# Masks on exponentials by a VectorE minimum, half projections and other fill slots in a five-stage attention kernel

## The chip, the cores and the metric

The kernel runs on one core of a Trainium2 chip. The metric is the device time in microseconds of one execution, the median of several. Engines are called PE (TensorE), ACT (ScalarE), DVE (VectorE), POOL (GpSimd) and SP (SyncE, which here only issues DMAs).

## What is computed

The input x is a batch of 8 sequences of 512 tokens and 256 channels, and a second tensor ctx of the same shape gives keys and values to some layers. Six attention layers follow one another. The first five have 16 heads of 16 channels each: stage 0 (keys from layer-normed ctx, an own 512x512 mask per sequence, then an MLP), stage 1 (keys from ctx, no mask that acts within the scores), stage 2 (keys from ctx, one mask for all sequences, then an MLP), stage 3 (self-attention, causal), stage 4 (keys from ctx, no mask, then an MLP). The sixth is the tail: 16 heads of 64 channels. Cut to one of the first five:

```python
q, k, v = heads(norm(x) @ wq + bq), heads(keys @ wk + bk), heads(keys @ wv + bv)
scores = einsum('bhqd,bhkd->bhqk', q, k) * 16 ** -0.5
scores = where(mask, -inf, scores)            # stages 0, 2, 3
x = x + einsum('bhqk,bhkd->bhqd', softmax(scores), v) @ wo + bo
x = x + gelu(norm(x) @ w1 + b1) @ w2 + b2     # stages 0, 2, 4
```

## The kernel before

**Units and bodies.** A unit is one sequence in one stage. The program is a chain of bodies, written per engine by `walk`. Each body works on three units at once: on `prev` it finishes the output projection (`y`), the residual and, where its stage is in `MLP`, the MLP; on `cur` it does the attention; on `nxt` it does the norm, the projections and the first row maxima. So a body whose `prev` has an MLP (an MLP body, 24 in all) differs from the others. Of the 40 bodies that have a `cur`, 16 have one of a masked stage (0 or 2): 14 of these are MLP bodies, and two (the first of either stage) are not. Nine more MLP bodies have an unmasked `cur` (the first of stages 1 and 3, seven of stage 4), and there are 14 plain bodies (seven of stage 1, seven of stage 3). In front stands a prelude without `cur`; after stage 4 come a body with only a `prev` and the tail, which the change does not touch.

**A step.** Attention is 16 steps in a body: four groups of four heads, four key tiles each. In step i PE computes the transposed scores of four heads, f32, into the four banks of `psT` (`exp_scores`, L639), adds in masked stages a penalty of -2^100 where the mask stands, by one more matmul per head with the identity as weights (L645; causal: L647), and ACT takes the exponential of two heads at a time into `probs` (L916). PE multiplies them by V one step later (`outputs`, L660), because `exp_scores` of step i has to wait until ACT has read step i-1 from `psT`.

**Maxima.** The subtracted row maxima come from a bf16 product into the two banks of `psS` (`max_scores`, L620) that DVE reduces: two 128x512 instructions that add a penalty row and take the maximum in masked and causal stages (L1087), one 128x1024 reduction elsewhere (L1090). There are 32 per unit. They run ahead of the attention by 16 or 24 (`LEADS`); `maxima_plan` says how many stand ahead of, beside and behind the other work of a step, and 16 stand inside the MLP.

**Fills.** All other products go through the single bank `small`, one fill after another: x and c (transposes of the normed x and ctx), q0, q1, k0, k1 (projections), v0, v1 (two token tiles each), m1 to m3 and m0 (maxima turned by a matmul), y0, y1, h0, h1 (transposes for the MLP), z. The tables `CUR_USES`, `Y_USES`, `NXT_USES` and so on give each fill its slot; slot 2i stands behind the scores of step i, slot 2i+1 behind its outputs. PE may write a fill only after an engine has read the one before: ACT takes x, c, h, q, k (L938, L947, L951), DVE takes v, m, y (L1108, L1110, L1114, L1120).

**Other queues.** ACT turns the uint8 masks of stage 0 into bf16 penalties (`penalties`, L955): one set at slot 17 or 15, one at the very end of the body. SP issues the loads of a body in order, then stores the heads' outputs, gathers them with their sums, and after DVE's reciprocal (slot 5) spreads the reciprocals (L472, L477); POOL then scales the gathered outputs (L1345), which y0 waits for.

## Time and profile before

| what | us |
|---|---|
| median of 3 runs (5240.43 to 5261.33) | 5246.33 |
| the profiled execution | 5242.84 |
| its span | 5241.0 |
| a typical stage 0 body (window 416 to 537) | 121 |
| a typical stage 1 body (window 1248 to 1315) | 67 |
| stage 4, five MLP bodies (window 3262 to 3810) | 548 |
| the tail (window 3970 to 5241) | 1271 |

A row of the timeline gives the start, the length, the engine and line, the operation with its tiles, and in square brackets how long the engine had been idle and what released it. A group row gives busy time, the mean of one instruction in ns, and behind the bar the idle time ahead of such instructions with its releasers. A matmul row counts two instructions for one f32 product.

### The profile page before, as it was taken

How to read it: one execution, taken by the hardware profiler on the slowest of the kernel's cores; microseconds unless marked ns; L12 is line 12 of the kernel's file. 1: busy time of each engine (PE TensorE's matmuls, PEld its weight loads, DVE VectorE, ACT ScalarE, POOL GpSimd, SP SyncE). 2: the span in 40 equal slices, each digit the busy share in tenths (PEclk: the TensorE clock that was granted, in tenths of full speed). 3: DMA queues.
4: the chain of work that ended last, by engine and by line, in shares of the span. 5: the costliest groups of instructions: out<-in, count | busy, mean ns of one | idle time of the engine just before them, and what ended most of it. 6: DMA issues, size and time to landing. Idle time of an engine off the chain costs nothing.

```text
span 5241.0 us, 69325 instructions
## 1 busy us (share of the span) xinstructions
PE 4666.1 (89%) x24708; PEld 1851.2 (35%) x24708; DVE 2678.7 (51%) x6305; ACT 2286.7 (44%) x2870; POOL 919.6 (18%) x831
## 2 busy tenths in 40 slices
PE   5899999898888999999888888888867999999999
PEld 2333333332332333343433333333333333333333
DVE  5544554457676444454455565444422545554554
ACT  3444444456564444434444444444432433333332
POOL 0111111101110111001111111110111433333333
PEclk8999999999999999999999999999988999999999
DMA  1111111121121100001111211110111000000000
GB/s 57 33 42 45 41 49 49 35 71 66 56 69 46 40 30 31 30 29 40 65 59 57 68 63 43 41 35 33 37 42 52 1 13 13 13 13 13 1 13 9
DMA packets 152319, 201.89 MB, mean 39 GB/s; under 512 B 18993, under 2 KB 102321, under 8 KB 150706
## 3 DMA queue, kind: packets, MB, share of 16 engines
q1 hardware_dynamic: 151986, 197.31, 11.1%
q8 instruction: 226, 3.70, 0.3%
q14 instruction: 107, 0.88, 0.1%
HBM read 128.86 MB, written 68.42 MB: 38 GB/s over the span
## 4 chain that ended last, share of the span: by engine, by line
PE 69%; issue 11%; DVE 9%; ACT 7%; DMA 2%; POOL 1%; SPq 1%; ACTq 0%; DVEq 0%; POOLq 0%
PE psT L639 8%; PE small L592 7%; PE psT L717 6%; PE psO L660 6%; PE small L599 6%; PE psS L620 6%; PE psT L859 4%; ACT probs L916 4%; PE psT L645 3%; PE psT L726 3%; PE small L726 3%; DVE out L1087 3%; PE psT L592 2%; PE psT L824 2%; PE psO L874 2%
## 5 line engine op out<-in xcount | busy, mean ns | idle before, releaser
L916 ACT ACTIVATE probs<-psT 128x1024 f32<-128x1024 f32 (+3 forms) x1280 | 1158.9, 958 | 1150.7 <-PE psT L645 541.4
L1090 DVE TENSOR_REDUCE nmb<-psS 128x2 bf16<-128x1024 f32 x512 | 627.5, 1226 | 438.6 <-PE psS L620 438.3
L639 PE MATMUL psT<-low 32*128 32x512 f32 (+3 forms) x5120 | 744.7, 610 | 103.3 <-ACT probs L916 74.6
L1087 DVE CUSTOM_DVE_ANT_0 out<-psS,pens_sb 128x512 f32<-128x512 f32 x1024 | 665.8, 688 | 106.3 <-issue 68.6
L620 PE MATMUL psS<-out 32*128 32x512 bf16 (+3 forms) x2560 | 485.8, 376 | 253.5 <-DVE nmb L1087 104.1
L660 PE MATMUL psO<-probs,V 128*32 128x512 f32 (+3 forms) x5120 | 664.0, 592 | 1.0 <-ACT probs L916 1.0
L1272 DVE TENSOR_REDUCE parts<-psS 128x2 bf16<-128x1024 f32 x256 | 314.9, 1230 | 522.1 <-PE psS L846 522.1
L1027 ACT ACTIVATE probs<-psT 128x1024 f32<-128x1024 f32 x256 | 262.0, 1023 | 526.1 <-PE psT L862 526.1
L620 PEld LDWEIGHTS psS<-out 32*128 32x128 bf16 x2560 | 121.3, 91 | 979.9 <-issue 330.7
L717 PE MATMUL psT<-out,W 128*128 128x512 f32 x768 | 382.3, 618 | 0.2
L1084 DVE MEMSET scratch<- 128x1 f32 x768 | 45.3, 59 | 636.0 <-PE psS L620 611.9
L1389 POOL TENSOR_TENSOR oN<-oN,probs 128x1024 f32<-128x1024 f32 x128 | 300.6, 2349 | 316.1 <-ACT probs L1027 315.8
L947 ACT ACTIVATE low<-small,vec 128x512 f32<-128x512 f32 x320 | 222.7, 748 | 229.9 <-PE small L592 228.3
L639 PEld LDWEIGHTS psT<-low 32*128 32x128 f32 x5120 | 236.4, 188 | 192.1 <-ACT probs L916 131.0
L1338 POOL TENSOR_TENSOR var<-mhalf 128x4 f32<-128x4 f32 x80 | 15.9, 198 | 1593.2 <-ACT low L947 1593.2
L859 PE MATMUL psT<-V 64*128 64x512 f32 x1024 | 290.0, 643 | 2.2 <-ACT parts L1017 1.0
L645 PE MATMUL psT<-pens_sb,identb 128*128 128x512 bf16 x1024 | 276.6, 394 | 0.0
L1087 DVE CUSTOM_DVE_ANT_0 out<-psS,tri_row 128x384 f32<-128x384 f32 (+3 forms) x512 | 230.4, 487 | 80.2 <-issue 69.6
L1114 DVE TENSOR_TENSOR low<-low,small 128x512 f32<-128x512 f32 x160 | 109.8, 687 | 303.7 <-PE small L699 301.9
L592 PE MATMUL small<-hT,Wqkv 128*128 128x512 f32 x448 | 226.6, 629 | 37.1 <-ACT hT L938 23.9
L961 ACT ACTIVATE gel<-psT,vec 128x512 f32<-128x512 f32 x192 | 131.9, 687 | 250.7 <-PE psT L717 250.4
L1389 POOL TENSOR_TENSOR oN<-probs 128x1024 f32<-128x1024 f32 x64 | 150.5, 2351 | 422.9 <-ACT probs L1027 422.9
(156 smaller groups left out, 5555.9 us busy)
## 6 DMA issues: line engine op xcount, KB each, us to landing
o_mid<-out SPq DMA_DIRECT2D x160, 256.0 KB, 2.0
oN<-o_mid SPq DMA_DIRECT2D x160, 128.0 KB
oN<-r_mid SPq DMA_DIRECT2D x80, 256.0 KB
x_mid<-xe SPq DMA_DIRECT2D x40, 512.0 KB, 2.9
xw<-x_mid SPq DMA_DIRECT2D x36, 512.0 KB, 4.1
xe<-x_mid SPq DMA_DIRECT2D x36, 512.0 KB, 4.8
cT<-ctxT SPq DMA_DIRECT2D x20, 512.0 KB, 4.2
W<-wm SPq DMA_DIRECT2D x6, 1024.0 KB, 8.1
```

What stands on the lines that cost most here:

```text
L592: last = nc.tensor.matmul(dst[:], w[:, c, cols], src[:, c, :], start=c == 0, stop=c == C - 1)
L620: last = nc.tensor.matmul(psS[e][:, 0:n], Qb[rows_of(j), q, a, c, qt * P:(qt + 1) * P], Kb[rows_of(j), q, c, 0:n], start=True, stop=True)
L639: last = nc.tensor.matmul(psT[j][:, q0:S], Kf[rows_of(j), q, a, c, kt * P:(kt + 1) * P], Qf[rows_of(j), q, a, c, q0:S], start=True, stop=p ...
L645: last = nc.tensor.matmul(psT[j], identb[:], pens[:, 1, kt * S:(kt + 1) * S], start=False, stop=True)
L660: last = nc.tensor.matmul(psO[32 * j:32 * j + 32, q0:S], V[:, u.parity, kt, head(g, j), :], probs[:, i % 2, j, q0:S], start=kt == 0, stop= ...
L717: last = nc.tensor.matmul(psT[m % 2], W1[:, c, m * P:(m + 1) * P], hM[:, c, :], start=c == 0, stop=c == C - 1)
L859: nc.tensor.matmul(psT[j], K5[n % 3][rows, kt * P:(kt + 1) * P], Q5[n % 3][rows, :], start=True, stop=False)
L916: nc.scalar.activation(probs[:, i % 2, two, q0:S], psT_all[:, two, q0:S], ACT.Exp, scale=float(DH) ** -0.5)\
L1087: nc.vector.tensor_tensor_reduce(junk[:, e, 0:n], psS[e][:, 0:n], penalty, 1.0, -3.0e38, ALU.add, ALU.max, nmb4[:, g % 2, qt, at:at + 1]). ...
L1090: nc.vector.tensor_reduce(nmb4[:, g % 2, qt, row:row + 33:32], psS_both[:, :, 0:n], AX, ALU.max)\
L1272: nc.vector.tensor_reduce(nmb[n % 2][:, qt, 0:P:DL], psS_both[:], AX, ALU.max, negate=True).then_inc(tail_s_read, 1)
L1389: nc.gpsimd.tensor_tensor(pacc[n % 2], before, P5[kt], ALU.add).then_inc(tail_summed, 1)
```

## The change

- `exp_scores`: in masked stages PE computes heads 2 and 3 first and signals them without a penalty; heads 0 and 1 follow and get theirs. Only two of four penalty matmuls remain. Causal steps keep all four.
- `limit` (DVE, new): the exponentials of heads 2 and 3 (128x1024 f32 in SBUF) are replaced by the minimum of themselves and a bf16 tile `lims` that is e^-64 where the mask stands and e^64 elsewhere. It stands at the head of DVE's next step, and `outputs` waits for it (semaphore `limited`). `limits` (ACT, new) makes the tile with one 128x2048 Exp.
- `outputs` of masked stages stand behind the late fills of their step.
- The penalties and the limit tile of stage 0 are made at slots 3, 5 and 7 in two buffers; the mask loads wait for three of them.
- Fills: q and k of non-MLP bodies come in two halves of 256 tokens each (q00, q01, ...); v comes as four fills of one token tile, two of them (v2, v3) in the next body at slots 1 and 3; y of non-MLP bodies comes as four single tiles; m1, m2, m3, m0, x0, x1 move, h0 and h1 are taken by DVE instead of ACT; in MLP bodies the maxima of step 12 stand beside and behind instead of ahead and beside. The row maxima have a buffer per group.
- SP: the loads of Wqkv and of cT wait until v3 has been taken, and stand behind the gather and ahead of `spread_recips`.

```diff
-CUR_USES = {True: {"m1": 1, "m2": 11, "m3": 17}, False: {"m1": 1, "m2": 10, "m3": 21}}
-Y_USES = {True: {"y0": 10, "y1": 12}, False: {"y0": 17, "y1": 19}}
-MLP_USES = {"h0": 18, "h1": 19, "z": 19.5}
-CTX_USES = {True: {"c0": 13, "c1": 14}, False: {"c0": 12, "c1": 12}}
-NXT_USES = {True: {"x0": 7, "x1": 8, "q0": 9, "k0": 16, "q1": 21, "m0": 22, "k1": 23, "v0": 25, "v1": 27},
-            False: {"x0": 7, "x1": 9, "q0": 11, "k0": 13, "q1": 23, "m0": 25, "k1": 27, "v0": 29, "v1": 31}}
-MASKS_AT = {True: 17, False: 15}
+CUR_USES = {True: uses_at("0 m1, 1 v2, 3 v3, 4 m2, 20 m3"), False: uses_at("0 m1, 1 v2, 3 v3, 12 m2, 20 m3")}
+Y_USES = {True: uses_at("10 y01, 12 y23"), False: uses_at("14 y0, 15 y1, 17 y2, 19 y3")}
+MLP_USES = uses_at("18 h0, 19 h1")
+CTX_USES = {True: uses_at("13 c0, 14 c1"), False: uses_at("10 c0 c1")}
+NXT_USES = {True: uses_at("6 x0, 7 x1, 9 q0, 16 k0, 21 q1, 23 k1, 24 m0, 27 v0, 29 v1"),
+            False: uses_at("6 x0, 7 x1, 9 q00, 10 q01, 11 k00, 13 k01, 21 q10, 23 q11, 25 k10, 26 m0, 27 k11, 29 v0, 31 v1")}
+MASKS_AT = (3, 5, 7)
...
-        last = (1, 1, 0) if out > IN_BLOCK else (0, 0, 0)
-        return [(0, 0, 0)] + 8 * [(1, 0, 0)] + 3 * [(0, 0, 0)] + 4 * [last]
+        last = [(0, 1, 1)] + 3 * [(1, 1, 0)] if out > IN_BLOCK else 4 * [(0, 0, 0)]
+        return [(0, 0, 0)] + 8 * [(1, 0, 0)] + 3 * [(0, 0, 0)] + last
...
-X_STATS, X_NORMALISE = (2, 3), (5, 6)
-C_STATS, C_NORMALISE = {True: (8, 9), False: (7, 8)}, {True: (11, 12), False: (10, 11)}
+X_STATS, X_NORMALISE = (2, 3), (5, 5)
+C_STATS, C_NORMALISE = {True: (8, 9), False: (6, 7)}, {True: (11, 12), False: (9, 10)}
...
+                if cur is not None and (new_keys or new_stage):
+                    wait_taken(sp, place, "cur", "v3")
+                if new_stage:
+                    sp.dma_start(Wqkv[:], wa[nxt.s, :, 0:N_QKV]).then_inc(qkv_in, 16)
+                if new_keys:
+                    sp.dma_start(cT[:], keys).then_inc(sem["ctx_in"], 16)
...
-                for j in range(4):
+                for j in (2, 3, 0, 1) if u.s in MASKED else range(4):
+                    plain = u.s != CAUSAL and not (u.s in MASKED and j < 2)
                     last = nc.tensor.matmul(psT[j][:, q0:S], Kf[rows_of(j), q, a, c, kt * P:(kt + 1) * P], Qf[rows_of(j), q, a, c, q0:S],
                                             start=True, stop=plain)
...
-                for j in range(4):
+                for j in range(2 if u.s in MASKED else 4 if u.s == CAUSAL else 0):
...
+                if i in (2, 3):
+                    wait_taken(pe, place, "cur", f"v{i}")
                 pe.wait_ge(sem["exp_done"], count("exp_done", u, 2 * i + 2))
+                if u.s in MASKED:
+                    pe.wait_ge(sem["limited"], count("limited", u, i + 1))
...
-                    long = any(use[0] in "qkvyw" for _, use in late)
+                    long = any(use in ("q0", "q1", "k0", "k1", "w") for _, use in late)
...
-                    if i == 0 and prev is not None:
-                        outputs(prev, STEPS - 1)
-                    if i > 0 and cur is not None and not after_mlp:
-                        outputs(cur, i - 1)
+                    of = prev if i == 0 else None if after_mlp else cur
+                    limited = of is not None and of.s in MASKED
+                    if of is not None and not limited:
+                        outputs(place, of, (i - 1) % STEPS)
...
                     for owner, use in late:
                         fill(place, owner, use, prev, cur, nxt)
+                    if limited:
+                        outputs(place, of, (i - 1) % STEPS)
...
-                if kind not in "xchqk":
+                if kind not in "xcqk":
...
+            def limits(u):
+                return nc.scalar.activation(masking(lims, u), masks[:, 1, :], ACT.Exp, bias=log_limit[:, 0:1], scale=-2.0 * LOG_LIMIT)
...
+                    if nxt is not None and nxt.s == 0 and slot == MASKS_AT[1]:
+                        score_penalties(nxt).then_inc(sem["pens"], 1)
+                    if nxt is not None and nxt.s == 0 and slot == MASKS_AT[2]:
+                        limits(nxt).then_inc(sem["pens"], 1)
...
-                if nxt is not None and nxt.s == 0:
-
-                    penalties(1).then_inc(sem["pens"], 1)
...
+            def limit(u, i):
+
+                dve.wait_ge(sem["exp_done"], count("exp_done", u, 2 * i + 1))
...
+                two, row = probs[:, i % 2, 2:4, :], masking(lims, u)[:, i % T * S:(i % T + 1) * S]
+                both = bass.AP(tensor=row.tensor, offset=row.offset, ap=[list(row.ap[0]), [0, 2], list(row.ap[1])])
+                nc.vector.tensor_tensor(two, two, both, ALU.min).then_inc(sem["limited"], 1)
...
                 for i, (before, beside, after) in enumerate(place.body.maxima()):
+                    of = prev if i == 0 else None if place.body.mlp and i == MLP_AFTER + 1 else cur
+                    if of is not None and of.s in MASKED:
+                        limit(of, (i - 1) % STEPS)
                     maxima(before)
```

## Rows read from the trace of the kernel before

**Rows 1.** The page: busy time of each engine.

```profile
PE 4666.1 (89%) x24708; PEld 1851.2 (35%) x24708; DVE 2678.7 (51%) x6305; ACT 2286.7 (44%) x2870; POOL 919.6 (18%) x831
```

**Rows 2.** Windows: length, busy PE, PEld, DVE, ACT, POOL, then granted clock, DMA.

```profile
416.00:537.00 121.00, 109.58 (x572) 45.47 (x576) 59.70 (x210) 56.78 (x65) 13.90 (x19) 0.98 0.12 41
...
1248.00:1315.00 67.00, 58.10 (x389) 20.10 (x388) 47.36 (x56) 40.80 (x48) 8.73 (x11) 1.00 0.19 65
...
1597.00:1694.00 97.00, 80.52 (x468) 27.16 (x469) 59.97 (x220) 41.27 (x48) 8.72 (x11) 0.95 0.17 56
...
3262.00:3810.00 548.00, 473.75 (x2480) 195.54 (x2478) 262.86 (x345) 249.34 (x300) 66.31 (x89) 0.98 0.11 38
```

**Rows 3.** Groups by line in the window 177 to 891, six masked MLP bodies.

```profile
L639 PE MATMUL psT<-low 32*128 32x512 f32 x768 | 114.6, 635 | 20.3 <-ACT pens_sb L955 11.8 <-ACT probs L916 7.6 <-DVE V L1110 0.7
...
L645 PE MATMUL psT<-pens_sb,identb 128*128 128x512 bf16 x384 | 103.7, 394 | 0.0
...
L620 PE MATMUL psS<-out 32*128 32x512 bf16 x386 | 75.0, 385 | 16.1 <-ACT out L951 12.6 <-DVE nmb L1087 3.5
...
L592 PE MATMUL small<-hT,Wqkv 128*128 128x512 f32 x48 | 23.8, 618 | 7.5 <-ACT hT L938 5.5 <-DVE xe L1152 2.0
...
L955 ACT ACTIVATE pens_sb<-out 128x2048 bf16<-128x2048 uint8 x12 | 23.0, 1917 | 0.0
L599 PE MATMUL small<-Wo,oN 128*128 128x256 f32 x96 | 23.0, 382 | 1.0 <-POOL oN L1345 1.0
...
L587 PE MATMUL small<-ident,xn 128*128 128x128 f32 x96 | 15.1, 280 | 5.4 <-ACT out L938 5.4
...
L1345 POOL TENSOR_TENSOR oN<-oN 128x1024 f32<-128x1024 f32 x6 | 14.1, 2350 | 56.3 <-DMA oN<-r_mid 56.3
...
L699 PE MATMUL small<-identb,nmb 128*128 128x128 bf16 x96 | 9.7, 225 | 6.2 <-ACT out L951 6.2
```

**Rows 4.** PE's timeline from the start of the body at 417.9.

```profile
417.90 1.14 PE L639 MATMUL psT<-low 32*128 32x512 f32 x8 [2.46 <-ACT pens_sb L955]
418.97 1.04 PE L645 MATMUL psT<-pens_sb,identb 128*128 128x512 bf16 x4
419.94 1.06 PE L660 MATMUL psO<-probs,V 128*32 128x512 f32 x8
...
425.39 1.14 PE L639 MATMUL psT<-low 32*128 32x512 f32 x8 [0.28 <-ACT probs L916]
...
429.18 1.14 PE L639 MATMUL psT<-low 32*128 32x512 f32 x8 [0.36 <-ACT probs L916]
```

**Rows 5.** Groups by form, DVE, whole span.

```profile
L1087 DVE CUSTOM_DVE_ANT_0 out<-psS,pens_sb 128x512 f32<-128x512 f32 x1024 | 665.8, 688 | 106.3 <-issue 68.6 <-DVE nmb L1087 36.7 <-DVE nmb L1090 0.6
...
L1131 DVE TENSOR_TENSOR valid<-valid,vtmp 128x512 f32<-128x512 f32 x1 | 0.7, 691 | 0.0
```

**Rows 6.** Timeline, SP and PE: the reciprocals are sent, and y0 starts.

```profile
428.48 0.34 SPq L472 DMA_DIRECT2D r_mid<-rsum  x1
...
441.39 1.89 PE L599 MATMUL small<-Wo,oN 128*128 128x256 f32 x8
```

**Rows 7.** PE's timeline in the window 3262 to 3375, stage 4.

```profile
3273.24 1.14 PE L639 MATMUL psT<-low 32*128 32x512 f32 x8 [0.79 <-ACT probs L916]
...
3280.40 1.98 PE L592 MATMUL small<-hT,Wqkv 128*128 128x512 f32 x4 [1.19 <-ACT hT L938]
3285.68 1.99 PE L599 MATMUL small<-Wo,oN 128*128 128x256 f32 x8 [2.12 <-POOL oN L1345]
...
3353.99 0.39 PE L620 MATMUL psS<-out 32*128 32x512 bf16 x2 [2.19 <-ACT out L951]
```

**Rows 8.** PE's timeline at the start of a plain stage 1 body.

```profile
1250.17 0.39 PE L620 MATMUL psS<-out 32*128 32x512 bf16 x2 [1.59 <-DVE V L1108]
...
1251.89 0.39 PE L620 MATMUL psS<-out 32*128 32x512 bf16 x2 [0.45 <-DVE nmb L1090]
```

**Rows 9.** The instructions that read `rstd`: duration ns min/median/max.

```profile
L1067 DVE TENSOR_SCALAR xn<-xw,mom,rstd x160: 390/410/860, 19.2 to 3714.7; 128x256 f32<-128x256 f32 x160
```

More of the change, by code:

```diff
@@ L178, in start, with named, first, last @@
         return self.i * self.step + self.before
+    def named(self, who, begins):
+        return [use for _, owner, use in self.body.uses if owner == who and use.startswith(begins)]
+    def first(self, who, begins):
+        return self.named(who, begins)[0]
+    def last(self, who, begins):
+        return self.named(who, begins)[-1]
 def schedule():
@@ L530, in _ @@
             sp.dma_start(W2[:], wm2[0]).then_inc(wm_in, 16)
-            for n, fills in enumerate(walk(sp, body)):
+            for n, _ in enumerate(walk(sp, body)):
                 s, kind = divmod(n - 1, 3)
-                if n >= 1 and s < 4 and kind == 1:
-                    sp.wait_ge(small_read, fills + 1)
-                    sp.dma_start(Wqkv[:], wa[s + 1, :, 0:N_QKV]).then_inc(qkv_in, 16)
                 if n >= 1 and s < 5 and kind == 0:
@@ L667, in fill @@
                 dst = small
-                kind, part = use[0], use[1:]
+                kind = use[0]
                 if kind == "x":
@@ L675, in fill @@
                     pe.wait_ge(sem["normed_m"], count("normed_m", u, 1))
-                if use == "k0" and u.s not in OWN_KEYS and u.s:
+                if kind == "k" and use == place.first(who, "k0") and u.s not in OWN_KEYS and u.s:
                     pe.wait_ge(sem["ctx_in"], count("ctx_in", u, 16))
                 if kind == "m":
-                    pe.wait_ge(sem["s_read"], count("s_read", u, 2 * T * (int(part) + 1) * reads(u.s)))
-                if use == "q0":
+                    pe.wait_ge(sem["s_read"], count("s_read", u, 2 * T * (int(use[1]) + 1) * reads(u.s)))
+                if kind == "q" and use == place.first(who, "q0"):
                     pe.wait_ge(qkv_in, 16 * (u.s + 1))
-                if use == "y0":
+                if kind == "y" and use == place.first(who, "y"):
                     pe.wait_ge(wo_in, 16 * (u.s + 1))
@@ L929, in take @@
                 u = {"prev": prev, "cur": cur, "nxt": nxt}[who]
-                kind, part = use[0], use[1:]
-                if kind not in "xchqk":
+                kind = use[0]
+                if kind not in "xcqk":
                     return
@@ L1195, in between, with mlp @@
                         normalise(1, xe, xn, halves(1)).then_inc(sem["normed_m"], 1)
-            def mlp(place, u, nxt):
+            def mlp(place, u, cur, nxt):
+                if cur is not None and cur.s in MASKED:
+                    limit(cur, MLP_AFTER)
                 for n in range(IN_BLOCK):
```

167 lines of the change are left out of this document (95 added, 72 removed).

## The prediction

> **What bounds the kernel now.** I read the page's busy times first: PE works for 4666.1 of the span's 5241.0 us, 89%, DVE half of it, ACT less [rows 1]. So PE is the path, and a change is worth what it takes off PE plus what it takes off PE's waits. The windows show that this holds in every kind of body, unequally [rows 2]: a masked MLP body has PE busy 109.6 of 121 us, a plain stage 1 body 58.1 of 67, the first body of stage 2 80.5 of 97, five bodies of stage 4 473.8 of 548. Then the groups of six masked MLP bodies, for what ends PE's waits [rows 3]: 20.3 us ahead of the scores (ACT making penalties or still at its exponentials), 16.1 ahead of the maxima, 7.5 + 1.0 + 5.4 + 6.2 ahead of fills, mostly for ACT to read `small`: 56.5 us, 9.4 per body. The timeline shows where steps carry no fill: scores 425.39, next scores 429.18, a period of 3.79 us with 0.36 of waiting, set by ACT's round, not by PE's work [rows 4].
>
> **The change, part by part.**
>
> *Penalties.* Two of four matmuls go in each of 16 x 16 = 256 masked steps. Four take from 418.97 to 419.94, so 0.2425 each by spacing [rows 4]; the group's 103.7 us for 384 gives 0.27 [rows 3]. I take 0.24, full-clock spacing: 0.48 a step, 7.7 a body. In the 14 masked MLP bodies PE is the path: 14 x 7.7 = -108. In the two masked bodies without MLP it mostly waits for DVE (16.5 of 97 us idle [rows 2]), so I count nothing there yet.
>
> *The minimum.* No row has a 128x1024 DVE operation with two SBUF inputs. Nearest is L1131, 128x512 f32 with both inputs in SBUF, 0.691 [rows 5]; twice that, 1.38, is a bound from above on its own engine. Adding 512 elements to L1087's pace is no less than 0.53 more (0.69 less a fixed part), so I take 1.2. From far above stands POOL's 128x1024 multiply of two SBUF tiles, 2.35 [rows 3]; from below 0.69, if the bf16 operand doubled the rate, for which no row speaks. DVE goes from 59.7 to 59.7 + 16 x 1.2 + 1.4 (two h takes) = 80 in a body of about 115. That fits, in sum. Queue order decides: `limit` of step i-1 stands at DVE's head of step i and needs only the first exponentials of step i-1, which finish a step earlier; the outputs that wait for it come after the scores and fills. In steps 1 to 8 one maximum (2 x 0.69 [rows 5]) and one limit a step leave room. Behind the MLP there are eight maxima in four steps: each then waits for a reduction with a limit in front.
>
> *Walk of a masked MLP body*, with 1.2 per limit, 1.38 per maximum, the other engines at their present pace, and the orders of the code; waits of PE that I get: step 0, v2 behind m1, which DVE takes after a limit, 0.8. Step 3, x1 must wait until ACT took x0, behind exponentials and (stage 0) a 1.92 penalty set [rows 3]: 1.9. y01: the reciprocals come at the end of a DVE stretch that now holds limits, v3, m2 and the whole normalisation, some 2.2 later after the scores of step 1 than now, while PE arrives 0.4 earlier; now y0 starts 12.9 after the reciprocals are sent, with almost no wait [rows 6], so 2.6. c0 right behind y23, without outputs between (seven bodies): 0.85. h1 behind h0: 0.85, as now. m3 and q1 behind the MLP: 0.3 + 0.8, against 0.3 (xe [rows 3]) and 0.6 now. Steps 12 to 15: m0 hides the take of k1, but the maximum behind step 12 and that ahead of step 13 stand back to back with a limit between: 0.55 + 1.5, then three of 0.6: 3.9, against 2.1 + 0.6 now (12.6 and 3.5 over six bodies [rows 3]). Gone is the 2.46 at the start of a body behind the penalties, and the 0.28 and 0.36 of steps 2 and 3 [rows 4], because the three new ACT sets lie under steps that now carry v3, m2, x0, x1. Sum 11.7 for stage 0, about 10.5 for stage 2; against 9.4, +2.3 with rounding up for stage 0: 14 x 2.3 = +32.
>
> *The two masked bodies without MLP.* They have 40 maxima; DVE busy is 60 of 97 [rows 2] and gets 19 more, in a chain where PE and DVE take turns. 79 plus the turns comes to about the present length: 7.7 less on PE and as much more waiting, 0, with -4 to +6 each.
>
> *Unmasked MLP bodies (9).* PE work stays. v2 and v3 fall into steps that wait 0.79 for ACT [rows 7]: -1.4. x0, x1 earlier take away q0's 1.19; y0's 2.12 shrinks by about 1 since 1.9 us of v stand ahead, though the reciprocals come 0.7 later; m2 at slot 4 and DVE taking h0 save about what the groups show for them in stage 0, 1.0 and 0.9 [rows 3]. Added: x1 0.65, q1 behind m3 0.8, the back-to-back maxima, while the 2.19 behind k1 [rows 7] falls to 1.0: +0.3 for the end. About -4; for hand-overs that I cannot see I take -3: -27.
>
> *Plain bodies (14).* One turn of maximum and reduction takes 1.72 (1250.17 to 1251.89 [rows 8]). A step has two gaps between maxima, about 1.15 (scores) and 1.4 (outputs and a maximum) of work [rows 4, 8]; each without a fill costs the rest. Half fills cover more gaps, but the long ones covered a gap with 1.9 of work that needed no cover; counting slots, 6.3 of waiting against 5.8. The 1.59 behind the V takes [rows 8] goes, as one tile takes DVE half; hand-overs of halves cost about 0.5, each half being read by ACT in instructions that cost more than half of a whole. -0.7 each: -10.
>
> *SP, POOL, prelude.* cT and Wqkv now wait for v3 and are issued with the reciprocals behind them. v3 is read at slot 3, the reciprocals come at slot 5, k0 and q0 later: hidden; were v3 late, the reciprocals and y would be. Mask loads wait for three sets, done at slot 7, well before SP arrives. POOL keeps its work; its scaling, late as computed, comes before the rstd of c, which DVE wants after y01: hidden. Prelude: one penalty set of 1.92 [rows 3] leaves the path ahead of the maxima and one joins it ahead of x0: 0. DMA volume is unchanged.
>
> Sum: -108 + 32 + 0 - 27 - 10 = -113. Against the profiled execution's 5242.84 (3.5 under the median of 5246.33, so no different within the runs): 5130.
>
> **A rule weighed.** The normalisation of xw has a median of 0.41 us but reaches 0.86 [rows 9], and POOL is at work for 13.9 us of a masked body [rows 2]; so DVE operations from SBUF can be stretched by up to 0.45 by something, with 16 limits a body added to them. If each of them paid that, DVE would get 7.2 a body more; PE's waits follow where DVE ends them, in about half of the steps: +3.6, times 16, +58. The Trainium skill, "SBUF — State Buffer", section "Who interferes with whom", says that a DVE instruction with two SBUF inputs and a GpSimd instruction that reads SBUF exclude each other for their whole length. By that rule the time would come out as in the second rival; the stretched normalisation fits it.
>
> **Rivals.**
> 1. *PE's waits go, too.* My walk assumes that DVE reaches each item as late as its queue allows. If the 3.9 at the end and the 2.6 at y01 don't arise, 14 x 6.5 = 91 more is gained: 5039. For it: every wait in rows 3 is short, and DVE idles half of the body. Against: eight maxima and four limits in four steps.
> 2. *The limits and POOL get in each other's way*, +58: 5188.
> 3. *Hand-overs of the halves.* Six further fills in 16 bodies without MLP cost a take each, as q0's 1.19 [rows 7] less its hiding, 0.9: 16 x 6 x 0.9 = +86 to 5216, and with half of rival 2 to 5245: no change that can be told.
> 4. *Slower: the limit takes 2.35, as POOL's operation of that shape does* [rows 3]. Then DVE has 99 of 115 us in a masked body and every step hangs on it: 1.15 x 16 more in DVE's row, 0.65 of it on the path in each step, 10 a body, and all 18 in the two others: 14 x 10 + 36 = 176, 5306. It decides from about 1.9 us per limit. For it only that row; against it L1131's 0.691 for half.
>
> The change does what it says: the dropped matmuls are 512 by the code.
>
> **How the numbers follow.** Forecast 0.50, rival 1 0.22, rival 2 0.15, rival 3 0.06, rival 4 0.07. A measurement here can tell about 0.5%, 26 us, so faster means under 5220: forecast, rivals 1 and 2: 0.87; same 0.06; slower 0.07. The forecast's own range is 5085 to 5180 (0.22 to 0.27 for a penalty matmul, -4 to +6 for the two bodies, 3 us a body on the walk). The range reaches from rival 1's value to a little over rival 2's, 5035 to 5200, and leaves out rivals 3 and 4 and the outer part of rival 1, 0.19.
>
> **What would show it.** The penalty group in the form 128x512 bf16 with 512 fewer instructions; a new DVE group of 256, about 1.2 us each; stage 0 bodies about 5 us shorter, stage 4 bodies 3 shorter, stage 1 within 1; no wait for penalties ahead of the scores; waits ahead of y01, and ahead of the maxima behind the MLP. I am wrong if the DVE group runs over 1.9, if outputs wait for it, or if masked bodies shrink by less than 2 or more than 9 us.

## The result and the profile after

| | before | after |
|---|---|---|
| median, us | 5249.88 (14 runs, 5240.43 to 5261.50) | 5230.91 (14 runs, 5217.12 to 5239.33) |
| the profiled execution | 5242.84 | 5238.51 |
| its span | 5241.0 | 5236.7 |
| mean granted clock of the span | 0.973 | 0.959 |

The ratio is 0.9962, interval 0.9953 to 0.9971: 19 us gained. The gain is small but clear of the scatter of the runs; it is within the 26 us that the prediction took as the least that can be told. 120 us were forecast (5130, range 5035 to 5200), so the prediction was wrong.

One sentence ahead of the prediction needs correction: by the code's `OWN_KEYS = (2, 3)` stages 2 and 3 both take their keys from x, so ctx feeds stages 0, 1 and 4, and a load of `cT` belongs to the units of stages 1 and 4.

The page of after: its busy line, the granted clock in 40 slices, and two of the groups.

```profile
PE 4648.7 (89%) x24484; PEld 1877.5 (36%) x24484; DVE 3017.8 (58%) x6690; ACT 2310.5 (44%) x3011; POOL 963.7 (18%) x831
...
PEclk9999999999999999999999999999988999999999
...
L1154 DVE TENSOR_TENSOR probs<-probs,parts 128x1024 f32<-128x1024 f32 x256 | 315.5, 1232 | 59.8 <-ACT probs L966 51.4
...
L642 PE MATMUL small<-Wo,oN 128*128 128x256 f32 x640 | 188.5, 435 | 81.8 <-POOL oN L1416 48.9
```

PE is busy 17 us less than in [rows 1], not 123, though DVE got what was forecast for it (+339: 316 of minima at 1.23 us each, and the takes of h). To see where, I cut both spans at the issues of the DMA that gathers the sums, one per body, 6 to 13 us into it. The windows of after, then of before; the columns are those of [rows 2]. In order: seven masked MLP bodies of stage 0; the first body of stage 1; seven plain bodies of stage 1; the first of stage 2; seven masked MLP bodies of stage 2; the first of stage 3; seven plain bodies of stage 3; the first of stage 4; seven MLP bodies of stage 4. Of before five of the nine are shown.

```profile
193.39:999.58 806.19, 728.64 (x3739) 300.25 (x3732) 550.98 (x1491) 381.49 (x436) 117.83 (x131) 0.96 0.13 42
999.58:1109.65 110.07, 93.58 (x481) 38.64 (x483) 47.24 (x67) 53.15 (x61) 12.72 (x17) 0.95 0.20 68
1109.65:1610.67 501.02, 434.00 (x2862) 165.78 (x2861) 341.93 (x482) 307.31 (x407) 61.02 (x77) 0.98 0.19 61
1610.67:1710.70 100.03, 77.08 (x460) 28.24 (x464) 78.43 (x240) 45.01 (x60) 10.66 (x11) 0.95 0.13 43
1710.70:2500.39 789.69, 719.55 (x3707) 293.41 (x3700) 525.80 (x1531) 345.79 (x407) 108.55 (x120) 0.97 0.10 35
2500.39:2598.18 97.79, 85.65 (x553) 42.17 (x551) 39.81 (x176) 38.21 (x58) 12.47 (x16) 0.97 0.19 66
2598.18:3058.77 460.59, 398.67 (x3289) 191.94 (x3292) 281.33 (x1218) 223.89 (x406) 61.08 (x77) 0.94 0.19 61
3058.77:3149.48 90.71, 73.34 (x426) 26.64 (x418) 55.37 (x64) 42.42 (x58) 8.74 (x11) 0.85 0.16 54
3149.48:3901.52 752.04, 655.32 (x3358) 272.82 (x3354) 347.82 (x468) 330.78 (x393) 88.26 (x117) 0.94 0.12 38
```

```profile
185.43:1011.79 826.36, 760.94 (x3970) 313.62 (x3962) 412.37 (x1363) 382.67 (x446) 96.16 (x131) 0.99 0.13 41
...
1119.17:1605.78 486.61, 426.63 (x2756) 150.03 (x2753) 344.45 (x472) 287.56 (x337) 61.11 (x77) 0.97 0.18 62
1605.78:1702.08 96.30, 80.17 (x476) 26.98 (x474) 59.12 (x217) 41.46 (x49) 8.72 (x11) 0.96 0.13 45
1702.08:2512.43 810.35, 750.09 (x3930) 308.20 (x3922) 388.99 (x1406) 355.59 (x422) 89.63 (x120) 0.99 0.10 34
...
3162.47:3908.12 745.65, 637.05 (x3348) 264.89 (x3348) 330.95 (x435) 338.99 (x405) 88.13 (x117) 0.98 0.11 38
```

The account of the two profiled executions, in us:

| bodies | forecast | came, by the windows | cut at the first scores |
|---|---|---|---|
| 14 masked MLP | -76 | (806.19 - 826.36) + (789.69 - 810.35) = -40.8 | -38.2 |
| 9 unmasked MLP | -27 | +2.7 (first of stage 1), -4.2 (first of stage 3), +6.4 (stage 4) = +4.9 | +1.5, -3.0, +7.8 = +6.3 |
| 14 plain | -10 | +14.4 (stage 1), -0.2 (stage 3) = +14.2 | +17.2, +0.2 = +17.4 |
| first of stages 0 (with the prelude), 2 and 4 | 0 | +8.0, +3.7, +3.4 = +15.1 | +4.9, +1.2, +2.0 = +8.1 |
| the rest | 0 | +2.3 | +2.3 |
| sum | -113 | -4.3 | -4.3 |

The last column cuts at the first scores of each body instead (179.05 before and 183.90 after for the second body of stage 0). It differs because the gather moves within the body: 6.4 us behind these scores in that body before, 9.5 after. So a row can be off by some 3 us, which matters for the single bodies more than for the stretches of seven.

**In masked MLP bodies** PE is busy 4.6 us less per body of stage 0 (32.3 / 7) and 4.4 of stage 2, where 7.7 was forecast, and idle 1.7 and 1.4 more (9.3 to 11.1, 8.6 to 10.0), where 2.3 was. The groups of PE in the seven bodies of stage 0, after, then before:

```profile
L682 PE MATMUL psT<-low 32*128 32x512 f32 x898 | 142.6, 657 | 5.2 <-issue 5.1
...
L663 PE MATMUL psS<-out 32*128 32x512 bf16 x450 | 90.0, 397 | 21.3 <-DVE nmb L1141 18.4 <-DVE nmb L1144 2.7
...
L688 PE MATMUL psT<-out,identb 128*128 128x512 bf16 x124 | 38.8, 396 | 0.0
L642 PE MATMUL small<-Wqkv,cT 128*128 128x256 f32 x112 | 36.6, 456 | 5.5 <-DVE low L1178 5.5
L688 PE MATMUL psT<-pens_sb,identb 128*128 128x512 bf16 x96 | 30.3, 399 | 0.0
```

```profile
L639 PE MATMUL psT<-low 32*128 32x512 f32 x896 | 133.6, 633 | 23.5 <-ACT pens_sb L955 14.0 <-ACT probs L916 9.3
...
L645 PE MATMUL psT<-pens_sb,identb 128*128 128x512 bf16 x440 | 118.2, 393 | 0.0
...
L620 PE MATMUL psS<-out 32*128 32x512 bf16 x450 | 87.4, 385 | 18.6 <-ACT out L951 14.7 <-DVE nmb L1087 3.5 <-DVE nmb L1090 0.3
...
L599 PE MATMUL small<-Wqkv,cT 128*128 128x256 f32 x112 | 27.9, 392 | 0.0
```

The penalties fell nearly as computed, from 118.2 to 38.8 + 30.3 us: 49 in seven bodies, 7.0 each. But the same scores take 9.0 more and the same 112 matmuls of v take 8.7 more, 456 ns each and not 392. The granted clock of these bodies went from 0.99 to 0.96. Not all of v's part belongs to the clock: in best2 (below), which has the new slots and a clock of 0.99, they take 32.1 us, so 4.2 of the 8.7 come with fills of one tile. The waits are others: ACT's 23.5 ahead of the scores is 5.2 now, and what ends the waits ahead of maxima and fills is mostly DVE. PE's timeline of after around the end of a stage 0 body, and below it the windows of the same stretch (PE's columns and, third from the end, the clock):

```profile
393.93 0.39 PE L663 MATMUL psS<-out 32*128 32x512 bf16 x2 [0.70 <-DVE nmb L1141]
395.89 0.61 PE L663 MATMUL psS<-out 32*128 32x512 bf16 x2 [1.57 <-DVE nmb L1141]
...
413.39 2.09 PE L682 MATMUL psT<-low 32*128 32x512 f32 x8 [2.58 <-issue]
...
417.65 2.07 PE L642 MATMUL small<-Wqkv,cT 128*128 128x256 f32 x4 [0.78 <-DVE low L1178]
```

```profile
394.00:397.00 3.00, 1.43 (x8) 0.76 (x12) 2.52 (x8) 0.00 (x0) 0.00 (x0) 0.70 0.45 129
397.00:400.00 3.00, 3.00 (x13) 0.59 (x6) 1.33 (x6) 1.74 (x2) 0.00 (x0) 0.50 1.02 350
...
412.00:415.00 3.00, 1.61 (x8) 0.52 (x8) 1.22 (x1) 0.00 (x0) 0.00 (x0) 0.54 0.03 8
415.00:418.00 3.00, 2.22 (x11) 1.00 (x8) 0.69 (x1) 1.94 (x2) 0.00 (x0) 0.50 0.00 0
```

Scores that take 1.14 us in [rows 4] take 2.09 at 413.39, at the 1.2 GHz level: the clock fell behind the 0.70 and 1.57 of waiting for maxima, and again behind the 2.58 at the start of the body. The second drop is not new, as before's body at 417.90 starts behind a wait of 2.46 [rows 4]. The first has grown. Windows of 3 us, each below full clock counted as (1 - clock) x 2 x its length, give the time at the lower level in seven masked MLP bodies:

| kernel | stage 0, us (per body) | stage 2, us (per body) |
|---|---|---|
| before | 20.5 (2.9) | 13.7 (2.0) |
| after | 68.3 (9.8) | 54.6 (7.8) |
| best1 (below) | 37.5 (5.4) | 37.5 (5.4) |
| best2 (below) | 20.5 (2.9) | 23.9 (3.4) |

In stage 0 a body spends 6.8 us more at half speed, some 3.4 us of work not done. By its size that covers the 3.1 which the 4.6 lacks against 7.7.

The start of the body is better than it looks in that one timeline. Before, units 2 to 7 of stage 0 (counted from 0) all begin behind a wait of 2.2 to 2.5 us for penalties, the 14.0 us of the group above. After, only units 3 and 5 do, 2.58 and 2.50 us with `issue` as the cause, the 5.1 above.

### The profile page after: what moved, and what is told of

Read it like the earlier page. It is cut to its first block, busy times and chain, and to the rows that moved or that the text cites. A ratio compares the mean times of both kernels' runs of the same rounds, so it can differ in the third digit from the quotient of the medians.

```text
span 5236.7 us, 70053 instructions
## 1 busy us (share of the span) xinstructions
PE 4648.7 (89%) x24484; PEld 1877.5 (36%) x24484; DVE 3017.8 (58%) x6690; ACT 2310.5 (44%) x3011; POOL 963.7 (18%) x831
## 4 chain that ended last, share of the span: by engine, by line
PE 64%; DVE 14%; issue 12%; ACT 4%; DMA 4%; POOL 1%; SPq 1%; DVEq 0%; ACTq 0%; POOLq 0%
PE psO L707 7%; PE small L635 7%; PE psT L764 6%; PE small L642 6%; PE psS L663 6%; PE psT L682 5%; PE psT L908 4%; DVE out L1141 3%; PE psT L773 3%; PE small L773 3%; DVE nmb L1144 3%; PE psT L635 2%; PE psT L873 2%; PE psO L923 2%; PE psT L642 2%
## 5 line engine op out<-in xcount | busy, mean ns | idle before, releaser
L682 PE MATMUL psT<-low 32*128 32x512 f32 (+3 forms) x5120 | 771.7, 621 | 49.7 <-ACT probs L966 28.2
L663 PE MATMUL psS<-out 32*128 32x512 bf16 (+3 forms) x2560 | 494.1, 383 | 219.1 <-DVE nmb L1141 121.4
L996 ACT ACTIVATE low<-small,vec 128x256 f32<-128x256 f32 (+1 forms) x464 | 262.2, 617 | 204.2 <-PE small L635 204.2
L1154 DVE TENSOR_TENSOR probs<-probs,parts 128x1024 f32<-128x1024 f32 x256 | 315.5, 1232 | 59.8 <-ACT probs L966 51.4
L682 PEld LDWEIGHTS psT<-low 32*128 32x128 f32 x5120 | 252.2, 192 | 145.8 <-issue 77.7
L635 PE MATMUL small<-hT,Wqkv 128*128 128x256 f32 (+1 forms) x656 | 242.9, 494 | 24.2 <-DVE low L1178 18.7
L642 PE MATMUL small<-Wo,oN 128*128 128x256 f32 x640 | 188.5, 435 | 81.8 <-POOL oN L1416 48.9
```

The source lines that it names most:

```text
L635: last = nc.tensor.matmul(dst[:, tokens], w[:, c, cols], src[:, c, tokens], start=c == 0, stop=c == C - 1)
L642: last = nc.tensor.matmul(dst[:, i * D:(i + 1) * D], src[:, c, t * P:(t + 1) * P], w[:, c, :], start=c == 0, stop=c == n - 1)
L663: last = nc.tensor.matmul(psS[e][:, 0:n], Qb[rows_of(j), q, a, c, qt * P:(qt + 1) * P], Kb[rows_of(j), q, c, 0:n], start=True, stop=True)
L682: last = nc.tensor.matmul(psT[j][:, q0:S], Kf[rows_of(j), q, a, c, kt * P:(kt + 1) * P], Qf[rows_of(j), q, a, c, q0:S], start=True, stop=p ...
L1154: nc.vector.tensor_tensor(two, two, both, ALU.min).then_inc(sem["limited"], 1)
```

## The experiments

All runs were compared with the kernel before on the same chip (medians 5252.6, 5255.3 and 5254.4 in three sessions). Each profile is one execution, and not always a middling one: after's is 7.6 us above its median, those of keys_behind and maxima_apart are 19 and 14 us below theirs. The lengths of bodies, in us, worked out from their profiles as above (stretches of seven divided by seven); where a slash stands, PE's idle time per body follows:

| bodies | before | after | before_two_pen | slots_only | limit_none | mask_only | dummy | best1 | best2 |
|---|---|---|---|---|---|---|---|---|---|
| prelude and first | 185.4 | 193.4 | 184.1 | 180.6 | 182.2 | 187.0 | 198.9 | 192.8 | 185.4 |
| stage 0 MLP | 118.1 / 9.3 | 115.2 / 11.1 | 116.4 / 13.4 | 115.0 / 6.1 | 114.5 / 11.0 | 119.3 / 16.1 | 121.0 / 8.6 | 113.1 / 10.8 | 113.1 / 5.1 |
| stage 1 plain | 69.5 | 71.6 | 69.2 | 71.0 | 71.0 | 69.0 | 71.6 | 71.9 | 70.8 |
| stage 2 first | 96.3 | 100.0 | 90.1 | 93.0 | 92.9 | 97.7 | 108.3 | 98.2 | 90.2 |
| stage 2 MLP | 115.8 / 8.6 | 112.8 / 10.0 | 113.9 / 12.7 | 115.4 / 6.5 | 111.3 / 9.7 | 119.3 / 16.3 | 120.0 / 7.5 | 111.6 / 10.1 | 113.2 / 5.5 |
| stage 3 plain | 65.8 | 65.8 | 66.0 | 65.7 | 65.8 | 66.1 | 65.7 | 65.4 | 65.3 |
| stage 4 MLP | 106.5 | 107.4 | 107.1 | 108.2 | 107.4 | 109.1 | 107.0 | 104.4 | 103.7 |

### The penalties alone, without a minimum or new slots

```diff
 # kernel before
-                plain = u.s not in (*MASKED, CAUSAL)
+                    plain = u.s != CAUSAL and not (u.s in MASKED and j < 2)
-                for j in range(4):
+                for j in range(2 if u.s in MASKED else 4):
```

(The signals for both pairs of heads follow the second penalty. So ACT starts on the first pair no sooner than before; in after it starts behind two scores.)

> The kernel before with the penalties of heads 2 and 3 left out and nothing in their place (their scores are not masked). It prices the removed matmuls alone. Theory 'clock': 512 matmuls at 0.24 us take 123 us off PE's row, but PE's waits keep their length and become a larger share, so the granted clock falls under 0.97 and a part is given back: 5150 to 5190. Rival 'waits alone': the clock stays at 0.97 and the whole 123 us come out: about 5127.

5218.33, ratio 0.9931 [0.9903, 0.9958]: 34 us gained of some 123, less than either theory had. The window of the seven stage 0 MLP bodies, and their scores:

```profile
184.07:998.55 814.48, 720.72 (x3746) 292.66 (x3742) 412.31 (x1361) 380.66 (x446) 96.15 (x131) 0.98 0.13 42
```

```profile
L639 PE MATMUL psT<-low 32*128 32x512 f32 x896 | 137.6, 653 | 36.8 <-ACT probs L918 21.4 <-ACT pens_sb L957 15.3
```

PE is busy 5.7 us less per body than before (40.2 / 7), idle 4.1 more, 28 in seven. Of these 28 us, 13.3 stand ahead of the scores (23.5 to 36.8), nearly all for ACT's exponentials (9.3 to 21.4); the rest stand ahead of fills and maxima, half of them for ACT as well. Over the whole span the waits ahead of the scores for `probs` rise from 74.6 to 100.6 us. So taking matmuls away uncovers ACT, whose round [rows 4] show for steps without a fill and which I had not carried into the term for the penalties. No minimum, no new slot and no other queue is touched here. But the first pair's signal stays where it was, so this run alone does not tell what after's new order of the pairs could have freed; the run without the minimum, below, does.

### The new slots alone

```diff
 # kernel after
-                for j in (2, 3, 0, 1) if u.s in MASKED else range(4):
-                    plain = u.s != CAUSAL and not (u.s in MASKED and j < 2)
+                for j in range(4):
+                    plain = u.s not in (*MASKED, CAUSAL)
...
-                if u.s in MASKED:
-                    pe.wait_ge(sem["limited"], count("limited", u, i + 1))
...
-                    limited = of is not None and of.s in MASKED
+                    limited = False
...
-                if cur is not None and cur.s in MASKED:
-                    limit(cur, MLP_AFTER)
```

(And the other call of `limit`, and ACT's order of the pairs.)

> The changed kernel with four penalty matmuls, no minimum, and outputs ahead of the late fills in every stage: the new slots and halves alone. Theory 'the slots cost in unmasked stages' (stage 1 and stage 4 bodies 2 us longer, as in the changed kernel): 5250 to 5280. Rival 'the minimum spoils it, the slots help': 5200 to 5230.

5230.32, ratio 0.9958 [0.9945, 0.9970]: the same as after. With the new tables the swap of two penalties a step for a minimum is worth nothing; it makes the masked MLP bodies 0.1 longer in stage 0 and 2.5 shorter in stage 2, and costs 12.8 in the prelude with the first body and 7.0 in the first body of stage 2 (9.7 and 4.3 if cut at the first scores).

### The minimum alone

```diff
 # kernel after, with the tables of the kernel before
-CUR_USES = {True: uses_at("0 m1, 1 v2, 3 v3, 4 m2, 20 m3"), False: uses_at("0 m1, 1 v2, 3 v3, 12 m2, 20 m3")}
+CUR_USES = {True: uses_at("1 m1, 11 m2, 17 m3"), False: uses_at("1 m1, 10 m2, 21 m3")}
...
-                    wait_taken(sp, place, "cur", "v3")
+                    sp.wait_ge(small_read, place.start() + 1)
```

(`Y_USES`, `CTX_USES`, `NXT_USES`, `maxima_plan` and the slots of the norms likewise. Three further parts of after stay: DVE takes h, the mask sets are made at slots 3, 5 and 7, and the outputs stand behind the late fills. SP's loads keep their new place behind the gather.)

> The changed kernel with the slots, whole projections, plan of maxima and order of normalisation of the kernel before, but with the minimum, half of the penalties and outputs behind fills. Theory 'the slots cost in unmasked stages': the unmasked stages have their old times, the masked bodies gain: 5190 to 5215, under the changed kernel. Rival 'the slots make room for the minimum': masked bodies gain nothing, 5240 to 5270.

5298.76, ratio 1.0085 [1.0060, 1.0111]: 46 us slower than before, which neither theory had. Masked MLP bodies idle 16 us. Not all of it is the minimum's: of the 59 us between the two profiled executions, 33 stand in the masked MLP bodies and 18 in stage 4, which has no minimum, so that part belongs to what else stays. Still, the slots are not an extra of the change but what makes the minimum bearable: slots alone 22 us faster, minimum without them 46 slower, both 19 faster.

### Idle work in place of the penalties

```diff
 # kernel after
+                if u.s in MASKED:
+                    for j in range(2):
+                        nc.tensor.matmul(psT[j], identb[:], masking(pensE, u)[:, kt * S:(kt + 1) * S], start=True, stop=True)
```

> The changed kernel with two idle 128x512 bf16 matmuls put back into each masked step, into banks that the scores overwrite (512 in all, 123 us of PE work). Theory 'clock': in masked bodies the granted clock rises from about 0.96 to 0.98 or more and the added work costs clearly less than itself, 40 to 80 us: 5270 to 5310. Rival 'the clock is no matter': the work adds in full, 5340 to 5355.

5343.21, ratio 1.0171 [1.0145, 1.0196]: 112 us slower than after, nearly the full 123. The clock of the stage 0 MLP bodies rose from 0.96 to 0.98, yet PE's busy time rose by 8.3 a body (787 against 729 in seven), more than the added 7.7. So a fuller PE does not pay for itself with its clock. And adding work costs nearly all of it while removing as much from before gave a third. That fits steps which stand near the point where PE's work and the round of the other engines are equal, a point that a row of busy times doesn't show. The two runs are not mirror images, though: the idle matmuls stand ahead of the scores, where they delay both pairs of exponentials, and the removed ones stood behind the first pair's signal. Idle work at that place was not tried.

### After without the minimum

```diff
 # kernel after
-                if u.s in MASKED:
-                    pe.wait_ge(sem["limited"], count("limited", u, i + 1))
...
-                if cur is not None and cur.s in MASKED:
-                    limit(cur, MLP_AFTER)
...
-                    if of is not None and of.s in MASKED:
-                        limit(of, (i - 1) % STEPS)
```

> The changed kernel without the minimum and without the wait for it (heads 2 and 3 stay unmasked); all else as it is. It prices the 256 minima. Theory 'DVE's queue': the waits of PE at fills that DVE reads and at the maxima behind the MLP shrink by 2 to 3 us a masked body and the granted clock there rises to 0.98: 5170 to 5195. Rival 'hidden': 5220 to 5235.

5202.61, ratio 0.9903 [0.9880, 0.9927]: the minimum costs 28 us by the medians. The first body of stage 2:

```profile
1591.93:1684.86 92.93, 76.33 (x468) 27.81 (x470) 60.66 (x226) 45.37 (x60) 8.68 (x11) 0.96 0.14 47
```

Against after that is 7.1 us less, with DVE busy 60.7 and not 78.4; the prelude with the first body loses 11.1. The masked MLP bodies lose only 0.7 (stage 0) and 1.5 (stage 2) each. In bodies with an MLP the minimum is nearly hidden; in the two without one, where DVE's 40 maxima and PE take turns, 0.44 to 0.70 us of each of the 16 minima lie on the path.

Beside slots_only this run prices the penalties once more, now in the new slots and with the first pair of heads signalled behind two scores: neither has a minimum, and one makes four penalties a step, the other two (the outputs stand behind the late fills in this one). The ratios to before are 0.9958 and 0.9903, 29 us for the same 512 matmuls: 0.6 us a body in stage 0 and 4.0 in stage 2. PE is busy 5.4 us less a body in stage 0 and idle 4.8 more. With this, -108 is out for the new order of the pairs as well.

### Half and whole fills

```diff
 # kernel after
-False: uses_at("14 y0, 15 y1, 17 y2, 19 y3")
+False: uses_at("17 y01, 19 y23")
...
-False: uses_at("6 x0, 7 x1, 9 q00, 10 q01, 11 k00, 13 k01, 21 q10, 23 q11, 25 k10, 26 m0, 27 k11, 29 v0, 31 v1")
+False: uses_at("6 x0, 7 x1, 11 q0, 13 k0, 23 q1, 26 m0, 27 k1, 29 v0, 31 v1")
```

> The changed kernel with q, k and y of the bodies without MLP whole again, in the slots of the kernel before; v stays in four tiles. Theory: each further fill costs PE about 0.1 to 0.15 us of restart and a hand-over: plain bodies 1.5 to 2 us shorter (71.6 to 70 in stage 1): 5195 to 5210. Rival: the halves were needed to cover the maxima: 5230 to 5250.

5250.76, ratio 0.9988 [0.9975, 1.0001]: 20 us worse than after. Plain bodies of stage 1 gain 1.2 (70.4), those of stage 3 lose 3.7 (69.5). The halves have a price and a use. The price stands in the groups of seven plain bodies, first before, then after:

```profile
L592 PE MATMUL small<-hT,Wqkv 128*128 128x512 f32 x64 | 31.7, 618 | 0.0
```

```profile
L635 PE MATMUL small<-hT,Wqkv 128*128 128x256 f32 x128 | 36.2, 405 | 0.5 <-ACT low L996 0.5
```

By busy time a half takes 0.283 us and half of a whole would be 0.248 (the means, 405 and 618 ns, include overlap): 4.5 us more for these, and 3.3 for k's products out of `cT`, in the same windows (23.8 to 27.1). y and v, which come a tile at a time, take 3.7 and 5.9 more. Other groups got shorter, so PE's busy time rose by 7.4 us in all (434.0 against 426.6); in this run, with v still in tiles, it is 422.0. The use is in stage 3, whose whole fills in the new slots uncover 3.7 us a body. Halves in stage 3 and wholes in stage 1 were not tried.

### Reciprocals ahead of the normalisation

```diff
 # kernel after, in DVE's `between`
+                if prev is not None and slot == RECIP_AT:
+                    reciprocals(prev)
...
-                if prev is not None and slot == RECIP_AT:
-                    reciprocals(prev)
```

> The changed kernel with DVE's reciprocals of slot 5 ahead of the normalisation instead of behind it. Theory: in MLP bodies PE waits at y01 for POOL's scaling (4.2 us in stage 4) and runs several us at half clock behind that wait; sent 2.65 us earlier, the wait shrinks by as much and the clock holds: 2 to 4 us a body in 23 MLP bodies, 5140 to 5185. Rival: x0 now waits longer for the norm, and the clock falls anyway: 5215 to 5235.

5229.63, ratio 0.9954 [0.9936, 0.9972]: nothing, and the wait of y for POOL is 49.3 us on the whole, as in after (48.9). The SP rows of one stage 4 body tell why; before, after, this kernel and the next one, keys_behind (the load of the keys `cT`, the gather of the outputs `oN<-o_mid`, the write of the reciprocals, their spread `oN<-r_mid`, which waits until the write has landed):

```profile
3365.26 0.37 SPq L512 DMA_DIRECT2D cT<-ctxT  x1
...
3384.08 2.33 SPq L467 DMA_DIRECT2D oN<-o_mid  x4
3388.14 0.34 SPq L472 DMA_DIRECT2D r_mid<-rsum  x1
3392.20 1.24 SPq L477 DMA_DIRECT2D oN<-r_mid  x2
```

```profile
3373.27 2.24 SPq L507 DMA_DIRECT2D oN<-o_mid  x4
3375.80 0.38 SPq L561 DMA_DIRECT2D cT<-ctxT  x1
3380.29 0.35 SPq L512 DMA_DIRECT2D r_mid<-rsum  x1
3383.23 1.25 SPq L517 DMA_DIRECT2D oN<-r_mid  x2
```

```profile
3363.82 2.23 SPq L507 DMA_DIRECT2D oN<-o_mid  x4
3366.35 0.38 SPq L561 DMA_DIRECT2D cT<-ctxT  x1
3368.00 0.35 SPq L512 DMA_DIRECT2D r_mid<-rsum  x1
3373.89 1.25 SPq L517 DMA_DIRECT2D oN<-r_mid  x2
```

```profile
3350.01 2.24 SPq L507 DMA_DIRECT2D oN<-o_mid  x4
3356.87 0.34 SPq L512 DMA_DIRECT2D r_mid<-rsum  x1
3358.34 1.25 SPq L517 DMA_DIRECT2D oN<-r_mid  x2
```

In after and in this kernel the spread goes out 7.4 and 7.5 us behind the load of `cT`, whether the small write is issued 4.5 or 1.7 us behind that load. Counted from the start of the gather (512 KB in four DMAs), the four bodies give 8.1, 10.0, 10.1 and 8.3 us, with the write sent 4.1, 7.0, 4.2 and 6.9 us behind it. The other bodies of before say the same: the write is sent 2.3 to 6.8 us behind the gather, and the spread follows the gather by 7.9 to 8.8. By these numbers the small write is waited for until what was queued ahead of it is through: the gather, in every kernel, and a load between the two adds 1.9 us. Sending the write earlier helps nothing.

### Keys behind the reciprocals

```diff
 # kernel after, MLP bodies
-                if new_keys:
+                if new_keys and not late_keys:
                     sp.dma_start(cT[:], keys).then_inc(sem["ctx_in"], 16)
...
+                if late_keys:
+                    if cur is not None:
+                        wait_taken(sp, place, "cur", "v3")
+                    sp.dma_start(cT[:], keys).then_inc(sem["ctx_in"], 16)
```

> The changed kernel with the load of cT (512 KB) in MLP bodies behind spread_recips instead of ahead of it. Theory: the write of the reciprocals lands only when the load ahead of it in the queue is through, 7.4 us after its issue; behind it, the scaling comes 3 to 4 us earlier in the eight MLP bodies whose next unit reads ctx (six of stage 4), y01 waits 1 us or none and the clock holds: stage 4 bodies 107.4 to about 103, total 5190 to 5207. Rival: POOL's scaling is late for other reasons, 5222 to 5235.

5226.60 (10 runs, 5207.99 to 5247.28), ratio 0.9946 [0.9930, 0.9963]. The stage 4 bodies fall from 107.4 to 105.2, and y's wait for POOL from 48.9 to 35.2 us on the whole. In stage 4 alone the wait went from 13.2 us before to 24.6 after, 1.9 for each of six bodies, and is 16.2 here. The mechanism is there, at 1.9 us a body and not the 3 to 4 expected; the whole time moved by 4 us only, within the intervals of the two.

### The maxima behind the MLP, and the first combination

```diff
 # kernel after
-        last = [(0, 1, 1)] + 3 * [(1, 1, 0)] if out > IN_BLOCK else 4 * [(0, 0, 0)]
+        last = 4 * [(0, 1, 1)] if out > IN_BLOCK else 4 * [(0, 0, 0)]
```

> The changed kernel with the maxima of steps 12 to 15 of MLP bodies all beside and behind, (0,1,1) four times, so that none stand back to back. Theory: the waits of 0.7 and 1.57 us and the half clock behind them go, 1.5 to 3 us a body in 21 bodies: 5170 to 5200. Rival: DVE paces these steps, the waits only move: 5220 to 5240.

5213.73, ratio 0.9920 [0.9904, 0.9937]: 17 us better than after. Stage 0 MLP bodies fall to 113.1, stage 4's to 105.4. The 1.57 shown above, a maximum directly behind another with a minimum between them on DVE, is what this order takes away: PE's waits ahead of maxima for DVE's masked reductions fall from 121.4 to 99.2 us over the span.

This order, the reciprocals first and whole fills together:

> The changed kernel with the three edits together: reciprocals first, maxima apart, whole q, k and y. If they are independent their gains add: by the theories about 5231 - 70 - 45 - 30 = 5085, at least 5150. Rival (each wait removed uncovers the next one): 5190 to 5230.

5220.79, ratio 0.9941 [0.9920, 0.9962]: worse than the order alone, as stage 3 loses 2.7 a plain body (68.5) again.

### Two versions for speed

Keys behind, maxima apart and reciprocals first, in one kernel:

> The changed kernel with three edits: cT behind the reciprocals, reciprocals ahead of the normalisation, maxima (0,1,1) behind the MLP. Theory: with cT out of the way the earlier reciprocals count, too: 5231 - 17 - 30 - 15 = 5170. Rival (no gain beyond the maxima): 5210.

5192.37, ratio 0.9878 [0.9849, 0.9906]: 38 us better than after, where the three alone gave 4, 17 and 1. What the other 16 come from is not settled (by the ratios to before, 44 against 8, 22 and 4, it is 10).

The same with four penalties a step and without the minimum (the edits of the slots alone):

> As best1, but with four penalty matmuls and no minimum. It tells what the minimum is worth once the other waits are gone. Theory: removing 123 us of PE work is worth 15 to 40 us only: 5185 to 5210. Rival (the minimum is worth nothing in net): equal to best1.

5170.64, ratio 0.9838 [0.9812, 0.9864]: 84 us below before by the medians, the fastest, and under what either theory had. Its windows of the seven MLP bodies of stages 0 and 2:

```profile
185.41:977.39 791.98, 756.37 (x3965) 314.10 (x3961) 420.57 (x1385) 383.79 (x437) 95.59 (x131) 0.99 0.13 43
...
1676.12:2468.34 792.22, 753.43 (x3930) 309.75 (x3929) 398.07 (x1418) 346.53 (x408) 88.67 (x119) 0.98 0.11 35
```

PE is busy as much as before (756 against 761 us in stage 0) at the same granted clock, and idle 5.1 us a body, not 9.3. Against best1 the MLP bodies are equal in stage 0 and 1.6 longer in stage 2; the prelude with the first body is 7.4 shorter and the first body of stage 2 8.0 (5.2 and 5.5 if cut at the first scores). The seven plain bodies of stage 1 and the seven of stage 4, which no minimum touches, are 12 us shorter in this profile too, for a reason that was not looked for. So the gain lay in the slots, and on top of the best of them the title's main part costs 22 us by the medians, of which its two bodies without an MLP show some 11.

## Why the prediction was wrong, step by step

- **Penalties, -108.** The step that failed first. The work that leaves is right: 7.0 us a body by the groups, 7.7 forecast. That "in the 14 masked MLP bodies PE is the path" is wrong downward: taken out of before alone, the work gave 34 us in place of 123, 1.7 and 1.8 a masked MLP body, and PE's idle time took up 4.1 of the 5.7 that it was busy less. In the new slots it gave 29. I had read the 0.36 and 3.79 of [rows 4] as a matter of steps without a fill and treated 7.7 as a pure gain in all of them.
- **PE's busy time at a constant clock.** 0.24 "full-clock spacing" was also taken as if the other matmuls kept theirs. They took 17.7 us more in seven bodies for scores and v alone; 4.2 of it came with v's smaller fills, the rest while the granted clock fell from 0.99 to 0.96. 6.8 us a body more at half speed, 3.4 of work, match the 3.1 between the 7.7 and the 4.6. The walk priced each wait at its length, and a wait that the clock follows costs more.
- **Walk of waits, +2.3 a body.** Near in size: +1.7 and +1.4 (its terms add up to 12.0, not 11.7). Several places fit as well: v2 behind m1 waits 0.78 (0.8 forecast), the maxima behind the MLP 0.70 and 1.57 (0.55 and 1.5). Others were wrong and made up for each other, so the sum owes something to luck: y01 waits 0.2 to 1.5 us in units 1 to 6 of stage 0 and not 2.6, with 4.9 in unit 7 alone; and the wait at the start of the body went in four of the six bodies that had it, and stayed in units 3 and 5.
- **The two masked bodies without MLP, 0, with up to +6.** They and the first of stage 4, which I had left out, came to +15, or +8 cut at the first scores. The run without the minimum puts 18 us of cost on the two (17 by that cut). "79 plus the turns comes to about the present length" was the error: in a chain of turns an instruction on one side adds itself, and the saved PE work did too little against it.
- **Unmasked MLP bodies, -27.** Came +4.9. "k0 and q0 later: hidden" looked at who reads the new keys. The load's harm was to what stands behind it in SP's order: the reciprocals, then POOL, then y, 1.9 us a body in stage 4. The prediction named the wait ahead of the load and not the load ahead of the write. "PE work stays" failed too: in stage 4 PE's idle time did fall, by 1.7 us a body where 3 was forecast, but its busy time rose by 2.6, with the clock at 0.94 and not 0.98 and v in single tiles.
- **Plain bodies, -10.** Came +14.2, all in stage 1. I priced the halves' takes at 0.5 and nothing for PE; PE is busy 7.4 us more in seven bodies, half of it, and idle 7.0 more. That the halves earn their place in stage 3 was not separated from stage 1 at all.
- **The minimum, 1.2 us.** Right: 1.232, 59.8 us of idle ahead of 256.
- **The rule weighed.** The timeline of after, POOL and DVE, around one of the few meetings of the two:

```profile
207.13 2.36 POOL L1416 TENSOR_TENSOR oN<-oN 128x1024 f32<-128x1024 f32 x1 [8.82 <-DMA oN<-r_mid]
...
207.37 3.20 DVE L1154 TENSOR_TENSOR probs<-probs,parts 128x1024 f32<-128x1024 f32 x1
```

  The minimum took 3.20 in place of 1.22, as if it had stood until POOL was through at 209.49 (209.49 - 207.37 + 1.22 = 3.34, nearly). In another body one that ran into the last 0.66 of POOL's took 1.75. Of the 256, these two took over 1.4. The Trainium skill, "SBUF — State Buffer", section "Who interferes with whom", says that the two exclude each other; the trace agrees where they meet, but the rival, in which each minimum pays, did not come: it cost 2.5 us in all. The normalisation paid more: its median over xw went from 410 [rows 9] to 664 ns, as slot 5 now puts all four tiles beside POOL's bias (four in 2.46 us at 308.21, next to POOL's 2.88 from 307.31). It reads one tensor and two columns of scalars, so the prediction was hasty to say that it fits a sentence on two SBUF inputs; the times show only that it is stretched where the two overlap. With the reciprocals ahead of it, it is 403 again, at no gain in time.
- **The rivals.** Rival 1 (waits go) is out. Rival 4 is out, as the minimum took 1.23. Rival 3 (5216 or 5245, hand-overs of the halves) lies around the time that came, but only by luck: 7 us of PE and as much of waiting in stage 1 are its mechanism, and in stage 3 it doesn't hold. None of them held the main cause, that work taken off a nearly critical PE is mostly not taken off the time.

## What to carry to other kernels

A busy share of 89% is no proof that work taken off that engine comes off the time: remove the work without its replacement and look at the time first; here that one run would have cut the largest term to a third. Price a moved DMA by what is queued behind it as well as by who reads it, a small write by what is queued ahead of it, and half-size fills by their own rows, not by half of the whole. When a change has a new idea and a new order of the slots, run them apart: here the order carried the gain and the idea cost 22 us on top of the best order.
